# A decoder layer's last stage regrouped: roots and small steps per group of chunks, rows scaled by ScalarE, and the experts' last rows sent tile by tile

## The reference

```python
def _layernorm(x, axis=-1, eps=1e-05):
    m = jnp.mean(x, axis=axis, keepdims=True)
    v = jnp.var(x, axis=axis, keepdims=True)
    return (x - m) / jnp.sqrt(v + eps)
...
    h = jax.nn.relu(jnp.einsum('enc,ech->enh', disp, ew1) + eb1[:, None, :])
    eo = jnp.einsum('enh,ehc->enc', h, ew2) + eb2[:, None, :]
    y = eo[ids_f, pos_c] * (probs_f * keep)[:, None]
    return y.reshape(Bx, Tx, K, Cx).sum(axis=2)
...
x = _layernorm(x + _L0_ffn_ref(x, ...), axis=-1)
```

## Time and profile before

| | |
|---|---|
| runs | 1882.13 us median of 3 (1882.13, 1885.53, 1870.05) |
| profiled execution | 1873.03 us, its span 1871.3 us |
| busy share of the span | TensorE 87%, VectorE 70%, ScalarE 53%, GpSimd 22% |
| mean granted TensorE clock | 0.92 of full speed |
| last stage | from 1827.9 us to the end of the span |
| in the last stage | granted TensorE clock 0.50, TensorE idle |

### The profile page before, as it was taken

How to read it: one execution, slowest core, us unless ns; L and a number is a source line. 1 busy time by engine, 2 the same in 40 slices (tenths; PEclk the granted TensorE clock), 3 DMA queues, 4 the chain that set the end, 5 groups by cost and what they waited for, 6 DMA issues and landing times. The chain is left out here.

```text
span 1871.3 us, 36268 instructions
## 1 busy us (share of the span) xinstructions
PE 1632.2 (87%) x14816; PEld 1064.6 (57%) x14816; DVE 1304.5 (70%) x2288; ACT 991.7 (53%) x1692; POOL 403.7 (22%) x268
## 2 busy tenths in 40 slices
PE   7858999999999999999584799879985999999970
PEld 7734444444444444444274555546764888888870
DVE  6967888888888888886185547652334677777736
ACT  5324777777777777777534267844533333333310
POOL 6540000000000000000234101101452244444440
PEclk9967999999999999999798679978996999999995
DMA  7887444544444444430455968223213333344235
GB/s 260 216 214 198 65 68 62 69 64 67 66 62 66 67 65 65 63 45 9 141 194 182 116 94 132 76 76 108 84 39 109 75 90 92 93 94 94 38 34 180
DMA packets 131133, 183.85 MB, mean 98 GB/s; under 512 B 30886, under 2 KB 95284, under 8 KB 129912
## 3 DMA queue, kind: packets, MB, share of 16 engines
q1 hardware_dynamic: 117528, 159.47, 40.6%
q0 software_dynamic: 13440, 22.07, 5.7%
HBM read 114.86 MB, written 69.99 MB: 99 GB/s over the span
## 5 line engine op out<-in xcount | busy, mean ns | idle before, releaser
L694 DVE TENSOR_REDUCE att_row_max<-att_ring 128x2 f32<-128x1024 f32 x512 | 602.2, 1220 | 115.8 <-PE att_ring L760 57.1
L678 ACT ACTIVATE att_w_exp<-att_s_ps 128x512 f32<-128x512 f32 x999 | 536.2, 599 | 222.4 <-PE att_s_ps L807 150.3
L834 PE MATMUL att_a_ps<-att_w_exp,att_v_group 128*32 128x512 f32 x2048 | 273.6, 606 | 0.8 <-ACT att_acc_sb L667 0.6
L793 PE MATMUL att_s_ps<-att_q_stack,att_k_stack 62*128 62x512 f32 x640 | 182.0, 481 | 0.0
L793 PEld LDWEIGHTS att_s_ps<-att_q_stack,att_k_stack 62*128 62x128 f32 x640 | 84.4, 184 | 124.0 <-ACT att_w_exp L678 112.9
L2232 ACT ACTIVATE ex_hid<-ex_h_ps,ex_b 128x512 f32<-128x512 f32 x128 | 87.2, 686 | 118.0 <-DVE ex_h_lo L2287 65.9
L616 POOL COPY att_eyes<-keep_slope_eye 128x384 bf16<-128x384 bf16 x16 | 8.1, 511 | 642.7 <-PE att_s_ps L807 631.9
L2188 POOL DMA_INDIRECT x_scr<-ex_y,ex_home x64 | 107.0, 1671 | 182.3 <-DVE ex_y L2277 167.6
L2287 DVE TENSOR_TENSOR ex_h_lo<-ex_hid,ex_h_hi 128x512 fp32r<-128x512 f32 x128 | 138.6, 1083 | 4.4
L760 PE MATMUL att_ring<-att_k_stack,att_q_stack 60*128 60x512 f32 x640 | 131.5, 451 | 6.2 <-DVE att_att L721 3.2
L807 PE MATMUL att_s_ps<-att_eyes,keep_past_bf 64*128 64x64 bf16 x3738 | 130.6, 193 | 0.0
(11 more groups left out here) (303 smaller groups left out, 3549.9 us busy)
## 6 DMA issues: line engine op xcount, KB each, us to landing
first_w_raw<-ew SPq DMA_DIRECT2D x16, 1024.0 KB
att_k_stack<-qk_scr SPq DMA_DIRECT2D x120, 128.0 KB
cr_q_stack<-q_scr SPq DMA_DIRECT2D x48, 256.0 KB, 9.6
keep_k_stack<-qk_scr SPq DMA_DIRECT2D x72, 128.0 KB
rows_scr<-att_zeros POOLq DMA_DIRECT2D x8, 1040.0 KB, 22.2
first_rows<-rows_scr SPq DMA_DIRECT2D x16, 520.0 KB
att_q_stack<-qk_scr SPq DMA_DIRECT2D x60, 128.0 KB
qk_scr<-qkv_t_hi SPq DMA_DIRECT2D x7, 1024.0 KB, 4.3
```

Source lines behind the costliest of these rows:

```text
L678: nc.scalar.activation(w_exp[(STEPS * g.n + st) % SETS][h][:, :], score_bank(v), ACT.Exp).then_inc(exp_done, 1)
L694: nc.vector.tensor_reduce(out, ring[place.slot][:, :, :], AX.X, ALU.max).then_inc(ring_free, 1)
L793: ins = nc.tensor.matmul(score_bank(v), ks[g.buf][rows, c, j, kt * P:(kt + 1) * P], qs[g.buf][rows, j, c * CH:(c + 1) * CH], start=True, s ...
L834: ins = nc.tensor.matmul(a_ps[32 * h:32 * h + 32, :], vg[g.buf][:, kt, h * VW:h * VW + 32], w_exp[(STEPS * g.n + st) % SETS][h][:, :], sta ...
```

## The change

In the experts stage, the last half (h = 15) leaves `send_home` and `scale_y`. VectorE scales each tile right after its bias and raises `scaled` per tile; GpSimd waits for the share steps and for `added` of the half before once, ahead of the first tile, and then for each tile's `scaled` before it issues that tile's transfer. All other halves stay.

In the last stage, `Norm` is replaced by code of its own. The chunks form five groups, (0, 1), (2, 3), (4, 5), (6) and (7). VectorE does the statistics of a group, then the small steps (`invert`) of the group before, then the aggregates and `var` of the group itself. A root and each small step cover a whole group (4 or 8 values a partition). A fifth small step makes `shift` = -mean * inv. ScalarE scales the rows as inv * x + shift, one ACTIVATE of a 128x256 tile with both operands per partition, and takes root k + 1 ahead of the rows of group k. Of the last chunk, VectorE scales tiles 2 and 3 itself, from mean and inv, and ScalarE tiles 0 and 1; the two halves go out as two transfers of 256 KB. Loads, buffers for chunks and the sizes of the other outputs are the same.

```diff
@@ -2194,7 +2194,13 @@
                 if e < E - 1:
                     split_weights(e + 1, (e + 1) % 2)
                 send_home(2 * e, 0)
-            send_home(2 * E - 1, 1)
+            h = 2 * E - 1
+            pool.wait_ge(share_step, SHARE_STEPS * (h + 1))
+            pool.wait_ge(added, 64 * h)
+            for t in range(TPC):
+                pool.wait_ge(scaled, h + t + 1)
+                pool.indirect_dma_start(io["x2_scr"], bass.IndirectOffsetOnAxis(home[h % 4][:, t, :], 0), y[1][:, t, :], None,
+                                        compute_op=ALU.add).then_inc(added, 16)
             pool.wait_ge(added, 64 * 2 * E)
 
         @block.scalar
@@ -2318,9 +2324,13 @@
             shares(0, 0)
             for e in range(E):
                 expert(e, e % 2, e == E - 1, e == 0)
+
+            h = 2 * E - 1
+            dve.wait_ge(share_step, SHARE_STEPS * (h + 1))
             for t in range(TPC):
-                bias_y(2 * E - 1, E - 1, 1, 1, t)
-            scale_y(2 * E - 1, 1)
+                bias_y(h, E - 1, 1, 1, t)
+                dve.wait_ge(biased, 4 * h + t + 1 + 4)
+                nc.vector.tensor_scalar(y[1][:, t, :], y[1][:, t, :], share[h % 4][:, t, :], None, ALU.mult).then_inc(scaled, 1)
 
         @block.tensor
         def _(pe):
@@ -2378,33 +2388,102 @@
 
 def stage_combine(nc, io):
 
+
+    groups = [(0, 1), (2, 3), (4, 5), (6,), (7,)]
+    group_of = {n: k for k, group in enumerate(groups) for n in group}
+    last = CHUNKS - 1
+
     with Scope(nc, "co") as s:
         x3 = [s.sb(f"x3{c}", [P, TPC, C], F32) for c in range(CHUNKS)]
         out = [s.sb(f"out{c}", [P, TPC, C], F32) for c in range(CHUNKS)]
-        norm = Norm(nc, s, io["apart"])
+        stats = s.sb("stats", [P, TT, 6], F32)
+        mv = s.sb("mv", [P, TT, 2], F32)
+        var, root, inv, half, shift = (s.sb(name, [P, TT, 1], F32) for name in ("var", "root", "inv", "half", "shift"))
         in_done = io["chunk_in"]
-        norm_done, out_done = s.sem("norm_done"), s.sem("out_done")
+        stats_done, mv_done, var_done, root_done = s.sem("stats_done"), s.sem("mv_done"), s.sem("var_done"), s.sem("root_done")
+        inv_step, rows_done, end_done, out_done = s.sem("inv_step"), s.sem("rows_done"), s.sem("end_done"), s.sem("out_done")
         block = s.block()
+
+        def tiles(k):
+            return slice(TPC * groups[k][0], TPC * groups[k][-1] + TPC)
 
         @block.sync
         def _(sp):
             for n in range(CHUNKS):
                 sp.dma_start(x3[n][:, :, :], chunk_rows(io["x2_scr"][0:T], n)).then_inc(in_done[n], 16)
-            for n in range(CHUNKS):
-                sp.wait_ge(norm_done, n + 1)
+            for n in range(last):
+                sp.wait_ge(rows_done, n + 1)
                 sp.dma_start(chunk_rows(io["out"], n), out[n][:, :, :]).then_inc(out_done, 16)
-            sp.wait_ge(out_done, 16 * CHUNKS)
+            sp.wait_ge(end_done, 1)
+            sp.dma_start(chunk_rows(io["out"], last)[:, 2:4, :], out[last][:, 2:4, :]).then_inc(out_done, 16)
+            sp.wait_ge(rows_done, last + 1)
+            sp.dma_start(chunk_rows(io["out"], last)[:, 0:2, :], out[last][:, 0:2, :]).then_inc(out_done, 16)
+            sp.wait_ge(out_done, 16 * CHUNKS + 16)
 
         @block.scalar
         def _(act):
-            for n in range(CHUNKS):
-                norm.take_root(act, n)
+            def take_root(k):
+                act.wait_ge(var_done, k + 1)
+                nc.scalar.activation(root[:, tiles(k), :], var[:, tiles(k), :], ACT.Sqrt).then_inc(root_done, 1)
+
+            def rows(n):
+                act.wait_ge(inv_step, 5 * group_of[n] + 5)
+                for t in range(2 if n == last else TPC):
+                    at = TPC * n + t
+                    ins = nc.scalar.activation(out[n][:, t, :], x3[n][:, t, :], ACT.Identity, bias=shift[:, at, :], scale=inv[:, at, :])
+                ins.then_inc(rows_done, 1)
+
+            take_root(0)
+            for k, group in enumerate(groups):
+                if k + 1 < len(groups):
+                    take_root(k + 1)
+                for n in group:
+                    rows(n)
 
         @block.vector
         def _(dve):
-            for n in range(CHUNKS):
+            def gather(n):
                 dve.wait_ge(in_done[n], STACKED + (ROUTED if n < 4 else 0) + 16)
-                norm.apply(dve, n, x3[n], out[n]).then_inc(norm_done, 1)
+                for t in range(TPC):
+                    ins = nc.vector.bn_stats(stats[:, TPC * n + t, :], x3[n][:, t, :])
+                ins.then_inc(stats_done, 1)
+
+            def moments(n):
+                wait_alone(dve, stats_done, n + 1, io["apart"])
+                for t in range(TPC):
+                    ins = nc.vector.bn_aggr(mv[:, TPC * n + t, :], stats[:, TPC * n + t, :])
+                ins.then_inc(mv_done, 1)
+
+            def spread(k):
+                dve.wait_ge(mv_done, groups[k][-1] + 1)
+                nc.vector.tensor_scalar(var[:, tiles(k), :], mv[:, tiles(k), 1:2], EPS, None, ALU.add).then_inc(var_done, 1)
+
+            def invert(k):
+                at = tiles(k)
+                dve.wait_ge(root_done, k + 1)
+                nc.vector.reciprocal(inv[:, at, :], root[:, at, :]).then_inc(inv_step, 1)
+                dve.wait_ge(inv_step, 5 * k + 1)
+                nc.vector.scalar_tensor_tensor(half[:, at, :], inv[:, at, :], -0.5, var[:, at, :], ALU.mult, ALU.mult).then_inc(inv_step, 1)
+                dve.wait_ge(inv_step, 5 * k + 2)
+                nc.vector.tensor_tensor(half[:, at, :], half[:, at, :], inv[:, at, :], ALU.mult).then_inc(inv_step, 1)
+                dve.wait_ge(inv_step, 5 * k + 3)
+                nc.vector.scalar_tensor_tensor(inv[:, at, :], half[:, at, :], 1.5, inv[:, at, :], ALU.add, ALU.mult).then_inc(inv_step, 1)
+                dve.wait_ge(inv_step, 5 * k + 4)
+                nc.vector.scalar_tensor_tensor(shift[:, at, :], mv[:, at, 0:1], -1.0, inv[:, at, :], ALU.mult, ALU.mult).then_inc(inv_step, 1)
+
+            for k, group in enumerate(groups):
+                for n in group:
+                    gather(n)
+                if k:
+                    invert(k - 1)
+                for n in group:
+                    moments(n)
+                spread(k)
+            invert(len(groups) - 1)
+            for t in (2, 3):
+                at = TPC * last + t
+                ins = nc.vector.tensor_scalar(out[last][:, t, :], x3[last][:, t, :], mv[:, at, 0:1], inv[:, at, :], ALU.subtract, ALU.mult)
+            ins.then_inc(end_done, 1)
 
 
 def consts():
```

## The result

The changed kernel took 1860.83 us in the median of 17 runs (1856.42 to 1871.15), the kernel before 1877.01 in 17 runs beside it (1869.5 to 1887.98). The ratio is 0.9915, 95% interval [0.9898, 0.9932]: 16 us, with 13 to 19 inside the interval. The prediction had said 13.0 us less, 1869.1 us, range 1855 to 1877, and had called it a step that one would most likely not be able to tell from none. The size holds, at the edge of the interval; that reading fails.

The account below looks back on a forecast made before the run. The prediction took VectorE's row work in the last stage, with the experts' tail ahead of it, to bound the kernel. Gains of 11.0 and 2.0 us sum to 13.0, from a median of 1882.13 to 1869.1 us, range 1855 to 1877.

Parts of the forecast that it names:

- The bound: Last stage: VectorE's eight chunks fill 36 of 43.4 us; ahead of it the experts' tail also lies bare on the path.
- VectorE's sum: Last stage: VectorE's statistics, aggregates, var and small steps before the last root sum to 19.4 us, with 0.3 for waits.
- ScalarE's line: Last stage: ScalarE scales 30 tiles at 0.48 us pitch, unbroken from the third chunk, and ends computing 1.1 us after VectorE.
- Outputs: Last stage: 1 MB queued from 1855.6 ends at 1860.3 (0.85 + 3.0 + 0.85 us); splitting the last piece gives little.
- The stage: Last stage: its end moves from 1871.3 to 1860.3, 11.0 us less.
- The experts' tail: Last half of the experts: GpSimd's late additions start 2.1 us earlier; 2.0 us booked after small waits.
- The landing at 2.3 us after the last issue: Experts' tail: additions of the half before land at most 2.3 us after their last issue at 1810.73, so by 1813.0.
- GpSimd starts at 1813.2: Experts' tail: GpSimd's first late addition starts at 1813.2 instead of 1815.32, 2.1 us earlier.
- Rival 1: Experts' tail: the landing of the half before is the real gate, experts gain 0, total 11.0 us, 1871.1; chance 15%.
- The sum: Whole kernel: 11.0 us from the last stage plus 2.0 from the experts' tail makes 13.0 us.
- From the sum to the chances: Whole kernel: a gain beyond 1% got 24%, within 1% 73%, slower by over 1% 3%.

Follow-up runs that it names:

- experiment 7: Changed kernel with the shift left out of ScalarE's last-stage rows (Identity became Copy): eight tiles in 3.28 us instead of 4.02, stage 29.5 us.
- experiment 8: Changed kernel with chunk 7 sent as one 512 KB transfer: 31.7 us from first load to end, against 31.6 and 31.3.
- experts_only: The experts' edit alone, last stage as in the kernel before: ratio 1.0018 to that kernel, end 57.1 us after VectorE's last bias against 58.0.
- experiment 4: Changed kernel, GpSimd waiting only for additions of the half before the previous one: ratio 0.9936 to the kernel before, first late send 0.13 us after VectorE's last bias.
- experiment 5: Changed kernel without GpSimd's share and landing waits ahead of the last half's first tile: the pause is still 2.70 us.
- experiment 6: The kernel of experiment 5 with half 14 sending only tiles 2 and 3: half 15's first send follows after 0.30 us, a 2.67 pause after the fourth send.
- experiment 10: Changed kernel with SyncE issuing all eight last-stage loads at the end of the experts' block: ratio 0.9946 to the kernel before, end 45.7 us after the bias.

## Why the prediction was right or wrong, point by point

- **The bound.** Right. Both tails lay bare; the last stage was VectorE's 4.5 us per chunk, and its edit alone brings 12.0 of the 12.5 us.
- **VectorE's sum.** Slightly too long: 4.8 us was booked per group of two chunks, 4.32 was measured. The aggregates of a second chunk pay no wait of their own, and statistics start before `var`'s record is over. The last `var` ended 22.3 us into the stage, not 23.7.
- **ScalarE's line.** Right in kind and in order: unbroken from the third chunk, VectorE waiting for the last root. The pitch is 0.49, booked 0.48; experiment 7 shows the 0.09 us per operand. The page ScalarE: Activation LUTs of the Trainium skill (What ACT_TABLE_LOAD costs) had come to 0.49, and this trace agrees. The same page's rule against multiplies on ScalarE (Rules for kernel authors) would have spoken against a change that gained 12 us: per tile it is right (VectorE's pitch was 0.33), but VectorE was the engine that was full.
- **Outputs.** Right. 0.85 in front, 1.5 per 512 KB, 0.85 behind gives 31.4 us from the measured issues (chunk 6's at 1861.1); by experiment 8 the split is worth 0.3 us at most.
- **The stage.** 11.0 booked, 11.8 and 12.0 in the two profiles; the missing part is VectorE's sum.
- **The experts' tail.** The mis-sized term: 2.0 booked, 0.7 measured (0.9 in `experts_only`). The landing at 2.3 us after the last issue was right to a tenth. The step that failed is "GpSimd starts at 1813.2", a start 0.2 us after that landing: the send came 1.5 us after it. Experiments 4 to 6 show a pause of 2.7 us after four sends in a row, which no row of before could show, as there the fifth send had VectorE to wait for. What fills either stretch stays open. Rival 1 (the landing gates it, nothing gained) was nearer in size. The landing does gate the changed kernel (experiment 4); in the kernel before it came too early to be what GpSimd waited for: half 14's last send ended at 1810.73, and 2.3 and 1.5 us more make 1814.5, while the send started at 1815.32, 0.46 after VectorE's last scale.
- **The sum.** 13.0 booked, 12.5 in the tails, 16 in the medians. That 13.0 is so near 12.5 is in part luck: the experts' term was 1.3 us too large and the stage's 0.8 too small, and the two errors cancel.
- **From the sum to the chances.** This is what failed as a forecast. "Runs between 1870.05 and 1885.53 for one kernel are wider than the step" is true of single runs, and "About 1% (18.8 us) is what a measurement of this kernel can tell from no change" was taken for a limit; 73% went to a step within 1%, read as no change that could be told. The measured 0.85% lies within 1%; what failed is that reading. With 17 runs of each the interval was 0.34% wide, and a step of 0.7% stands clear of it. The chances should have followed the mechanism: all likely cases of the sum gained, none lost.
- **The spread itself** was left unexplained. The one profile of before could not show it; side by side the experiments' profiles do: the cross-attention stage takes 243.1 to 256.2 us at granted clocks of 0.79 to 0.75, while attention stays at 799 to 802. Why the clock differs from execution to execution is open.

## What to carry to other kernels

Compare tails from an event just ahead of them: here 12.5 us of gain appeared as 5.4 between two spans, mostly because an untouched stage had run at a lower clock. When steps of one engine are handed to another, look at the order in that engine's queue: here the last root stood behind eight tiles and VectorE waited 2.52 us for it. With the root ahead and four more tiles on VectorE, ScalarE was done 2.3 us earlier, and the next bound (the queue of outputs) took 1.5 of it back. A step smaller than the spread of single runs is not a step that cannot be measured: ask how many runs stand behind a median before giving chances to "no change".

## What the runs showed of the hardware that was not expected

- Scattered additions issued by GpSimd go out at a pitch of 1.85 us, four in a row; before the fifth there is a pause of 2.66 to 2.70 us though every semaphore that it waits for is there (experiments 4, 5). It does not belong to the border between halves (experiment 6); whether it goes by the count or ends with the landing of the fourth is not shown.
- SyncE's issue of a 512 KB load takes 0.37 to 0.5 us while few are under way, and 1.3 to 1.4 us each from the sixth on: eight took 7.4 us (experiment 10). Loads issued ahead of a block's end can so hold the block.
- GpSimd's drain at the end of a block with scattered additions took 2823 ns in both kernels (1824.8 before, 1831.3 after) and with loads running beside it.
